# A two-unit loop for the second attention, with all nine key blocks of a group weighed in one burst

## What is computed

```python
xn = layernorm(x, ln_x_g, ln_x_b)              # 77 context rows
ln = layernorm(latents, ln_l_g, ln_l_b)        # 1024 tokens
q  = (ln @ Wq)                                 # 16 heads of 64
kv = concatenate([xn @ Wkv, ln @ Wkv], axis=1) # 1101 keys
qn = rmsnorm(q, qn_g) * scale
kn = rmsnorm(k, kn_g)
attn = softmax(einsum('bhid,bhjd->bhij', qn, kn))   # padded context keys masked
out  = einsum('bhij,bhjd->bhid', attn, v)
return out @ Wout + bout
```

## Time and profile before

| What | Value |
|---|---|
| Runs shown | median 2195.23 us of 3 (2191.35 to 2196.08) |
| Profiled execution, its own time | 2200.02 us |
| Its span in the profile | 2198.2 us |
| PE busy | 1955.0 us (89%) |
| DVE busy | 1254.4 us (57%) |
| ACT busy | 1002.8 us (46%) |
| POOL busy | 607.8 us (28%) |
| Median landing of a key spread (`a_KHL`) / query spread (`a_QHL`) after issue | 4.6 us / 2.3 us |

### The profile page before, as it was taken

The page is one execution under the profiler, slowest core; times in us unless marked ns, Lnnn a source line. Parts: engine busy times, 40 slices in busy tenths (PEclk is TensorE's granted clock), DMA queues, the critical chain, the costliest instruction groups (busy, mean ns, idle before and its releaser), DMA issues. The chain is left out here.

```text
span 2198.2 us, 40034 instructions
## 1 busy us (share of the span) xinstructions
PE 1955.0 (89%) x13656; PEld 1661.2 (76%) x13657; DVE 1254.4 (57%) x2963; ACT 1002.8 (46%) x1747; POOL 607.8 (28%) x555
## 2 busy tenths in 40 slices
PE   4888957999579999999999999999999984799994
PEld 2477947999467887787778887877778764799994
DVE  5273064677647766676677676767666656122223
ACT  2543414555245555554555555555555541344441
POOL 2300002333144432442244323432343100222220
PEclk9898958999669999999999999999999995899997
DMA  5501163111322112211221122212211207311113
GB/s 196 172 35 73 62 233 105 47 48 48 110 68 68 42 38 59 68 40 31 68 69 39 39 60 68 49 29 62 69 40 36 56 1 271 125 36 38 33 38 127
DMA packets 93663, 159.24 MB, mean 72 GB/s; under 512 B 22385, under 2 KB 54831, under 8 KB 91707
## 3 DMA queue, kind: packets, MB, share of 16 engines
q1 hardware_dynamic: 82875, 134.32, 21.6%
q0 software_dynamic: 8320, 20.65, 3.1%
q10 hardware_dynamic: 2304, 2.10, 0.3%
HBM read 71.57 MB, written 32.41 MB: 47 GB/s over the span
## 5 line engine op out<-in xcount | busy, mean ns | idle before, releaser
L1873 DVE TENSOR_REDUCE a_part_peak<-a_slot 128x1 f32<-128x512 f32 (+1 forms) x512 | 354.7, 732 | 315.0 <-PE a_slot L1689 314.5
L1832 ACT ACTIVATE a_probT<-a_slot 128x640 f32<-128x640 f32 x256 | 180.4, 705 | 474.8 <-PE a_slot L1698 251.3
L1689 PEld LDWEIGHTS a_slot<-a_KHL,a_QHL 128*128 128x128 f32 x1536 | 271.8, 190 | 121.8 <-issue 53.2
L1689 PE MATMUL a_slot<-a_KHL,a_QHL 128*128 128x512 f32 (+1 forms) x1536 | 343.7, 359 | 22.2 <-DVE a_probT L1896 11.9
L1820 ACT ACTIVATE a_prob<-a_slot,a_npeak 128x1024 f32<-128x1024 f32 x256 | 284.2, 1110 | 3.0 <-DVE a_npeak L1875 3.0
L1714 PE MATMUL a_po<-a_probT,a_V 128*64 128x256 f32 (+1 forms) x2304 | 276.8, 385 | 0.0
L1698 PE MATMUL a_slot<-ident,a_prob 128*128 128x128 f32 x2048 | 266.3, 273 | 0.0
L1698 PEld LDWEIGHTS a_slot<-ident,a_prob 128*128 128x128 f32 x2048 | 235.2, 142 | 8.4
L1714 PEld LDWEIGHTS a_po<-a_probT,a_V 128*64 128x64 f32 (+1 forms) x2304 | 153.6, 136 | 87.0 <-issue 21.5
L1639 PE MATMUL a_side<-a_W,a_latT 128*128 128x128 f32 x1536 | 205.9, 286 | 12.5 <-DVE a_KT L1883 6.6
L1639 PEld LDWEIGHTS a_side<-a_W,a_latT 128*128 128x128 f32 x1536 | 191.9, 201 | 18.8 <-DVE a_KT L1883 11.2
(11 more groups left out here) (319 smaller groups left out, 2989.0 us busy)
## 6 DMA issues: line engine op xcount, KB each, us to landing
a_KHL<-a_KT SPq DMA_DIRECT2D x128, 256.0 KB, 4.6
a_QHL<-a_QT SPq DMA_DIRECT2D x128, 128.0 KB, 2.3
m_up<-_L_ffn_gate_up_proj_dram SPq DMA_DIRECT2D x8, 1024.0 KB, 9.8
m_up<-in_L_ffn_W_dram SPq DMA_DIRECT2D x8, 1024.0 KB, 8.6
m_down<-in_L_ffn_W_dram SPq DMA_DIRECT2D x8, 1024.0 KB, 12.5
a_prob_dram<-a0p_zeros SPq DMA_DIRECT2D x4, 1632.0 KB, 11.0
a_dist_dram<-a_dist SPq DMA_DIRECT2D x4, 1632.0 KB, 8.2
a_band_prob<-a_prob_dram SPq DMA_DIRECT2D x4, 1632.0 KB, 6.8
```

Source lines behind the costliest of these rows:

```text
L1689: ins = t_.matmul(out[:, lo:hi], q, KHL[:, pair.parity, h, part, lo:hi], start=part == 0, stop=part == 1)
L1832: a_.activation(probT[:, u // 4 % 2, HALF:KT_TILES, h, u % 2 * P:(u % 2 + 1) * P], slot[u % 2][:, HALF * P:KT_TILES * P].rearrange("p (t q ...
L1873: v.tensor_reduce(part[:, i:i + 1], slot[u % 2][:, lo:hi], AX.X, ALU.max).then_inc(part_peaked, 1)
```

## The change

The loops of PE, ACT and DVE over the units become loops over steps of two units. In a step that begins with the even unit u, PE turns unit u, projects an output tile, turns unit u + 1, scores units u + 2 and u + 3, in every second step weighs a whole group, and then does the pieces. The table `FRONT` now names the first and `BEHIND` the second piece of a step. PE waits for `exped` of unit u + 1 ahead of the projection. ACT copies both units' second halves, then does the two exponentials; the step's first piece leaves `side` between the two exponentials where u is a multiple of 4, and behind both otherwise; its second piece comes last. DVE does both copies, both row sums, the inversion, both peaks, a bound and, last, its share of a piece. The order of pieces changes (Ktc before Qta, Qtb before V2), and with it SP's: the four transfers of Ktc are issued ahead of those of the first half of the queries.

```diff
-PIECES = ["Ka", "Kb", "c", "Qa", "Qb", "Kta", "V0", "Ktb", "V1", "Qta", "Ktc", "V2", "Qtb", "V3"]
-FRONT = {3: "c", 7: "Kta", 9: "Ktb", 11: "Qta", 13: "Qtb"}
-BEHIND = {0: "Ka", 2: "Kb", 4: "Qa", 6: "Qb", 8: "V0", 10: "V1", 11: "Ktc", 12: "V2", 14: "V3"}
+PIECES = ["Ka", "Kb", "c", "Qa", "Qb", "Kta", "V0", "Ktb", "V1", "Ktc", "Qta", "Qtb", "V2", "V3"]
+FRONT = {0: "Ka", 2: "c", 4: "Qb", 6: "Kta", 8: "Ktb", 10: "Ktc", 12: "Qtb", 14: "V3"}
+BEHIND = {0: "Kb", 2: "Qa", 6: "V0", 8: "V1", 10: "Qta", 12: "V2"}
...
 # SP
                 spread_keys(pair, "Ktb")
+                spread_keys(pair, "Ktc")
                 spread_queries(pair, 0)
-                spread_keys(pair, "Ktc")
                 spread_queries(pair, 1)
...
 # PE
-                for u in range(UNITS):
+                for u in range(0, UNITS, 2):
...
-                    if after and u in FRONT:
-                        piece(after, FRONT[u])
                     pe.wait_ge(exped, pair.g * UNITS + (u + 1))
-                    if u % 2 == 1 and two_before[0]:
-                        project_outputs(*two_before, u // 2 % 2)
                     if u % 4 == 2 and one_before[0]:
                         turn_sums(*one_before)
                     turn(pair, u)
-                    if one_before[0] and u % 2 == 1:
-                        weigh(*one_before, u // 2 % 2)
+                    pe.wait_ge(exped, pair.g * UNITS + (u + 2))
+                    if two_before[0]:
+                        project_outputs(*two_before, u // 2 % 2)
+                    turn(pair, u + 1)
+                    for k in range(2):
+                        nxt = ahead(pair, u + k, 2)
+                        if nxt[0]:
+                            pe.wait_ge(probT_act, pair.g * UNITS + (u + k + 1))
+                            pe.wait_ge(probT_dve, pair.g * UNITS + (u + k + 1))
+                            score(*nxt)
+                    if one_before[0] and u % 4 == 2:
+                        for part in range(len(PARTS)):
+                            weigh(*one_before, part)
+                    if after and u in FRONT:
+                        piece(after, FRONT[u])
                     if after and u in BEHIND:
                         piece(after, BEHIND[u])
-                    nxt = ahead(pair, u, 2)
...
 # ACT
             exponentials(start, 0)
+            exponentials(start, 1)
...
+                for u in range(0, UNITS, 2):
+                    copy_rest(pair, u)
+                    copy_rest(pair, u + 1)
+                    first, second = ahead(pair, u, 2), ahead(pair, u, 3)
+                    if first[0]:
+                        exponentials(*first)
+                    if after and u in FRONT and u % 4 == 0:
                         piece(after, FRONT[u])
...
+                    if second[0]:
+                        exponentials(*second)
+                    if after and u in FRONT and u % 4 == 2:
+                        piece(after, FRONT[u])
                     if after and u in BEHIND:
                         piece(after, BEHIND[u])
...
 # DVE, the new order of a step (normalise at u % 4 == 0 and copy_sums at u % 4 == 2 stand ahead of it)
                     copy_first(pair, u)
+                    if two_before[0]:
...
+                        add_outputs(*two_before, u // 2 % 2)
+                    copy_first(pair, u + 1)
                     row_sum(pair, u)
-                    if u % 4 == 3:
+                    row_sum(pair, u + 1)
+                    if u % 4 == 2:
                         invert(pair, u // 4)
...
+                    for k in range(2):
+                        nxt = ahead(pair, u + k, 2)
+                        if nxt[0]:
+                            peak(*nxt)
                     if after and u in BOUND_AT:
                         bound(after, BOUND_AT.index(u))
+                    if after and u in FRONT:
+                        piece(after, FRONT[u])
```

More of the change, by code:

```diff
@@ L1985, in body @@
                         normalise(*two_before)
[L1986 to L1992, removed]
                     if u % 4 == 2 and one_before[0]:
@@ L1996, in body @@
                     copy_first(pair, u)
+                    if two_before[0]:
+                        if isinstance(pair.g, int) and pair.g == 0 and u == 8:
+                            dve.wait_ge(based, 1)
+                        dve.wait_ge(turned, (pair.g * UNITS + u + 1) * 3 + 1)
+                        add_outputs(*two_before, u // 2 % 2)
+                    copy_first(pair, u + 1)
                     row_sum(pair, u)
-                    if u % 4 == 3:
+                    row_sum(pair, u + 1)
+                    if u % 4 == 2:
                         invert(pair, u // 4)
[L2000 to L2004, removed]
+                    for k in range(2):
+                        nxt = ahead(pair, u + k, 2)
+                        if nxt[0]:
+                            peak(*nxt)
                     if after and u in BOUND_AT:
                         bound(after, BOUND_AT.index(u))
+                    if after and u in FRONT:
+                        piece(after, FRONT[u])
             all_pairs(dve, body)
```

## The result

The changed kernel takes 2413.11 us (median of 4 runs, 2411.08 to 2418.18) against 2195.65 us; the ratio is 1.0997, with an interval of 1.0973 to 1.1020. The direction was right; the size, +217 us where +97 was predicted, lies outside the forecast's 2265 to 2320 us and outside the wider range that stands behind the chances, 2245 to 2335 us. One of the signs that the prediction named for being wrong came too: the clock of the loop is 0.93 and not 1.00.

What follows compares the result with a forecast made beforehand. PE was taken to set the pace; a pair would go from 72.29 to 78.7 us (68.6 work, 10.1 stalls), 15 × 6.45 = 97 us more, 2292 us; forecast 2265 to 2320, wider range 2245 to 2335.

Steps and rivals of the forecast that it cites:

- the signs that the prediction named for being wrong: Pairs at 72 us or less, loop clock under 1.00, scores waiting for `a_probT`, or first exponential much before 6.4 us.
- part 1: Weighing a whole group in one burst on PE: 4.04 us for 36 records, gaining 0.25 us a group, 1.0 a pair.
- part 3: Two pieces side by side through one PSUM bank: PE idles 0.60 to 1.41 us between them; stalls 10.1 us a pair.
- the wait for the second exponential at u = 6: PE in front of the projection (L1731), because Qb leaves `side` ahead of that exponential: about 1.06 us.
- the one behind Qtb: PE at u = 12, before V2: Qtb to 5.22 us, emptied from 6.42, + 0.78, so V2 from 7.2.
- part 2: Two-unit step through DVE and ACT: first exponential ready at 6.42 us; with a weighing, the second ends at 9.3.
- two row sums about 0.3 each: DVE, between the second unit's copy and the peaks: about 0.3 us each, first peak beginning at 3.4 us.
- POOL's work is unchanged: POOL in the loop: idle for two thirds of it, listed among the parts that cost nothing.
- 1.16 at worst: Copy in DVE's inversion; with the reciprocal before it, it puts peaks 1.35 us later in steps with a weighing.
- the sum: A pair takes 78.7 us (68.6 work, 10.1 stalls) against 72.29; 15 pairs × 6.45 = 97 us lost.
- a rival with a chance of 0.11: Clock falls in the stall at u = 8: 3.5 us more a pair, 53 in all, 2345 us; chance 0.11.
- the break-even: PE stalls of 3.66 us a pair (72.29 − 68.6), where the new order would neither win nor lose.

Runs made afterwards that it cites:

- the gaps filled: Changed kernel with idle transposes (30, 18 and 16) on PE between the two pieces of the steps u = 6, 8 and 12: 2332.26 us, ratio 1.0628.
- the spaced kernel: Changed kernel with row sums behind the peaks and each step's first piece ahead of both scores, second behind the weighing: 2180.47 us, ratio 0.9934.
- the version with one wait less: Kernel with row sums behind the peaks and pieces apart, DVE's share of Kta moved behind the next step's normalisation: 2158.11 us, ratio 0.9848.
- the three steps of POOL: Changed kernel with POOL's key scaling, square of the queries and its folds cut to two columns: 2328.00 us (one run).

## Why the prediction went wrong in size

**Right: part 1.** One burst is 4.04 us (1197.31 to 1201.35), as worked out. That its gain depends on the two-unit step, because the half bursts covered copies, was not in the prediction.

**Right: part 3.** The gaps between neighbours have the sizes of the earlier trace rows where DVE is on time: 0.69 behind Ka, 0.67 behind Ktc, 1.42 behind Kta once POOL's instructions are cut. With the two missed things removed, the change takes 2289 us against 2292 predicted. Some of that closeness is luck: the wait for the second exponential at u = 6 was reckoned 0.62 us too long and the one behind Qtb 0.45 too short, and they nearly cancel.

**Wrong: part 2, the chain through DVE.** The first step that failed is "two row sums about 0.3 each". It took the duration of one row for all units. At u = 6 they measured 1.95 and 1.70, and the weighing, which the prediction let cover the exponentials there, no longer did: the gap behind Kta was 4.24, not 1.41 beyond its last record. The trace of the kernel before had the warning, in the view of the row sum's line (shortest, median and longest in ns):

```profile
L1905 DVE CUSTOM_DVE_ANT_0 a_masked<-a_prob,a_maskf,a_latent_sum x256: 291/292/1655, 644.7 to 1803.9; 128x77 f32<-128x77 f32 x128
```

There they stand behind the peaks and copies, and the view names nobody who waited for them. The change moved them onto the chain, and the prediction priced POOL at nothing since "POOL's work is unchanged". The copy of the inversion, which it took at "1.16 at worst", was such a hold already: without POOL's instructions none of the 64 takes more than 0.33 us.

**Wrong: the clock, put at nothing.** The second step that failed is in the sum: it has every stall at a clock of 1.00, though the longest, 2.6 us, lay between a gap that had kept the clock and one that had lost it. The fall was a rival with a chance of 0.11, placed behind one gap a pair. It does not hang on the held row sums alone: with them freed, the gap at u = 8, which then had the size foreseen, brought it down in 10 pairs of 15, the one at u = 12, 0.45 us longer than foreseen, in all, and the run took 2328 us, above the forecast's 2320. That rival's price was 53 us for one gap a pair; in the changed kernel the clock fell behind three gaps a pair and cost 81 us, so 1.8 us a gap where 3.5 was reckoned.

How the 220 us between 2193.16 (the kernel before, run beside the last kernels) and 2413.11 divide depends on the order in which the two are taken away. The pieces and the chain as predicted cost 96 us (2289.39 − 2193.16) either way, near the 97 of the sum. With the gaps filled, the held row sums cost 43 (2332.26 − 2289.39), and the clock then 81 (2413.11 − 2332.26). The other way round, the clock costs 39 with the row sums freed (2328.00 − 2289.39), and holding them 85 (2413.11 − 2328.00): 43 as time, and 42 as clock that the longer gaps bring down. These are differences of medians, one of them a single run and some from different chips, so each is good to a few us; that they add up to the whole is so by construction and proves nothing.

**Right: the break-even.** 3.66 us of stalls a pair was given as the point from which the new order wins. In the pairs with pieces, PE's four repeated waits come to 2.5 us a pair in the spaced kernel and to 1.5 in the version with one wait less, and both win; with the row sums ahead of the peaks they come to 4.9, and it loses.

## What to carry to other kernels

Before an instruction is moved onto a chain, look at the longest of its kind and not at the median: a long tail that hides today is a price tomorrow, and the row of another engine that runs at that time says whose it is. Price a gap on PE twice, once as time and once as what the clock takes afterwards, and where its length lies between one that kept the clock and one that lost it, let the range hold both. And where all work of a kind leaves through one PSUM bank, put something between two fillings of it: here the gaps between neighbours were a loss of their own. But it was not enough: the two-unit step loses 10% with neighbours side by side, 2% with them apart, and wins 0.7% to 1.5% only when the row sums stand behind the peaks as well.

## What the runs showed of the hardware

DVE's row sum, which reads two tensors in SBUF, took 1.95 and 1.70 us in place of 0.29 beside two of POOL's instructions on tensors of 1152 and 1024 columns, and ended 0.1 us behind each; a reduction of one tensor beside such an instruction takes its 0.23 us. The Trainium skill says so ("SBUF — State Buffer", section "SBUF: two separate sides"): VectorE and GpSimd share a pair of SBUF ports, the one that starts first keeps it for its whole instruction, and a VectorE instruction with two SBUF inputs is among those that ask for it. The traces here agree for these rows: POOL's instruction had started 0.27 and 0.29 us before the row sum. They do not agree for all of POOL's work. Beside its power of 18 columns, 3.23 us long, the row sum of the kernel before took its 0.29:

```profile
666.22 3.23 POOL L1570 TENSOR_TENSOR a_kinv<-a_kvar,a_expo 128x18 f32<-128x18 f32 x1 [2.34 <-DVE a_kvar L1890]
...
666.66 0.29 DVE L1905 CUSTOM_DVE_ANT_0 a_masked<-a_prob,a_maskf,a_latent_sum 128x77 f32<-128x77 f32 x1
```

Two inputs are not needed for a hold either. The copy of the inversion reads one tensor; it takes 0.29 us alone, up to 1.15 in the changed kernel and at most 0.33 without the three steps of POOL (shortest, median, longest in ns, the changed kernel first):

```profile
L1925 DVE COPY a_rwide<-a_rsum x64: 293/294/1150, 647.4 to 2013.7; 128x256 f32<-128x256 f32 x64
L1934 DVE COPY a_rwide<-a_rsum x64: 293/294/331, 647.3 to 1930.5; 128x256 f32<-128x256 f32 x64
```

A gap of 2.20 us in the kernel before left the clock at 1.00. Gaps of 2.2 to 2.6 us were followed by a stretch at the lower level in all 30 cases of the changed kernel and in 25 of 30 without POOL's instructions; with the row sums behind the peaks, 8 of 16 gaps of 2.3 to 2.4 us were. So the length of a gap alone doesn't decide it; what else does was not settled.
